# Routing of token tiles and the first part's scatters moved into the attention's slots

## The reference

```python
h = tokens(x, W, b, gamma, beta)                 # 36 patch tokens an image: shifted patches, linear, layer norm; width 192
h = concatenate([h, weight[x_txt]], axis=1)      # 68 tokens an image, 2176 in all
h = h + attention(layernorm(h))                  # 12 heads, each query keeps its 32 best keys
n = layernorm(h)
logits_fk = (n @ W_fk + b_fk) @ normed(emb_fk).T # 128 experts
logits_rk = (n @ W_rk + b_rk) @ normed(emb_rk).T # 128 experts
w_fk, w_rk = top 4 of softmax(logits), divided by their sum
g = sum over the 4 experts e of w_fk[e] * (n @ f_know[e])      # 192 -> 128
y = sum over the 4 experts e of w_rk[e] * (g @ r_know[e])      # 128 -> 192
return h + y
```

## Time and profile before

| | |
|---|---|
| median of 3 executions | 988.81 us (983.92 to 992.14) |
| the profiled execution | 984.25 us, of it the span of the trace 982.4 us |
| TensorE busy, weight loads | 794.3 us (81%), 643.7 us (66%) |
| VectorE | 677.0 us (69%) |
| ScalarE | 324.5 us (33%) |
| GpSimd | 553.8 us (56%) |
| mean granted TensorE clock | 0.847 of 2.4 GHz |
| moved by DMA | 177.19 MB, 180 GB/s in the mean |

### The profile page before, as it was taken

How to read it: one execution, slowest core, us unless ns; L and a number is a source line. 1 busy time by engine, 2 the same in 40 slices (tenths; PEclk the granted TensorE clock), 3 DMA queues, 4 the chain that set the end, 5 groups by cost and what they waited for, 6 DMA issues and landing times.

```text
span 982.4 us, 21622 instructions
## 1 busy us (share of the span) xinstructions
PE 794.3 (81%) x6343; PEld 643.7 (66%) x6343; DVE 677.0 (69%) x4161; ACT 324.5 (33%) x887; POOL 553.8 (56%) x764
## 2 busy tenths in 40 slices
PE   5789999999999999988662288899998699589800
PEld 3778888888888777755441266799976458455800
DVE  2199999999999999984788179885453254255423
ACT  0134334444444344434631011233321146434700
POOL 5256566665666565643547475004775777775075
PEclk9789889998999789975755579999997799889955
DMA  9233453534343346301372496456799798489533
GB/s 331 93 135 129 161 184 112 180 127 163 129 168 114 112 136 219 122 23 34 93 183 71 143 289 226 154 141 176 208 393 409 266 317 297 142 293 367 180 100 92
DMA packets 81578, 177.19 MB, mean 180 GB/s; under 512 B 12952, under 2 KB 38232, under 8 KB 78648
## 3 DMA queue, kind: packets, MB, share of 16 engines
q1 hardware_dynamic: 56088, 120.62, 37.1%
q10 hardware_dynamic: 14112, 32.12, 8.8%
q0 software_dynamic: 11264, 23.09, 7.6%
HBM read 94.25 MB, written 81.53 MB: 179 GB/s over the span
## 4 chain that ended last, share of the span: by engine, by line
DVE 34%; PE 28%; POOL 17%; issue 13%; DMA 5%; ACT 1%; SPq 1%; POOLq 0%; DVEq 0%; ACTq 0%
DVE work L1356 12%; DVE top L1350 9%; PE bank L1216 6%; POOL early L742 5%; PE bank L1199 4%; PE bank L1214 4%; POOL slots_g L749 3%; POOL slots_x L720 3%; PE bank L1264 3%; PE bank L1266 2%; DMA early<-slots_x 2%; DVE s_hit L1520 2%; PE bank L1250 2%; PE bank L965 1%; DVE place L1626 1%
## 5 line engine op out<-in xcount | busy, mean ns | idle before, releaser
L1356 DVE MATCH_REPLACE8 work<-top,work 128x68 f32<-128x68 f32 x896 | 179.3, 211 | 0.0
L1350 DVE MAX8 top<-work 128x8 f32<-128x68 f32 x896 | 128.9, 213 | 6.6 <-ACT tru L792 6.2
L1626 DVE COPY place<-bank 96x512 f32<-96x512 f32 x98 | 66.0, 685 | 82.3 <-PE bank L1199 81.6
L742 POOL DMA_INDIRECT early<-slots_h,s_all x68 | 65.6, 964 | 87.4 <-DMA slots_h<-m_y 67.0
L1635 DVE COPY place<-bank 128x256 f32<-128x256 f32 x98 | 40.9, 423 | 92.8 <-PE bank L1250 91.5
L965 PE MATMUL bank<-early,xp 128*128 128x192 f32 x432 | 94.0, 381 | 6.5 <-DMA xp<-in_a_x 5.0
L965 PEld LDWEIGHTS bank<-early,xp 128*128 128x128 f32 x432 | 90.5, 233 | 8.6 <-DMA xp<-in_a_x 5.3
L742 POOL DMA_INDIRECT early<-slots_y,s_all x68 | 66.3, 975 | 52.7 <-DMA slots_y<-m_y 30.5
L1199 PE MATMUL bank<-ident,early 128*96 128x128 f32 x392 | 68.2, 301 | 25.4 <-DMA early<-slots_x 25.4
L672 POOL TENSOR_TENSOR sc<-work,tru 128x476 f32<-128x476 f32 x32 | 38.0, 1189 | 87.5 <-ACT work L827 87.5
L720 POOL DMA_INDIRECT slots_x<-early,s_all x68 | 67.7, 996 | 31.6 <-issue 18.4
(11 more groups left out here) (187 smaller groups left out, 1729.5 us busy)
## 6 DMA issues: line engine op xcount, KB each, us to landing
early<-slots_x SPq DMA_DIRECT2D x49, 384.0 KB
slots_y<-m_y ACTq DMA_DIRECT2D x49, 384.0 KB
slots_h<-m_y ACTq DMA_DIRECT2D x49, 256.0 KB
early<-slots_g SPq DMA_DIRECT2D x49, 256.0 KB, 4.8
f_all<-in_f_know SPq DMA_DIRECT2D x16, 768.0 KB, 9.8
r_all<-in_r_know SPq DMA_DIRECT2D x16, 768.0 KB, 15.3
slots_x<-zero SPq DMA_DIRECT2D x28, 360.0 KB, 3.0
slots_x<-zero SPq DMA_DIRECT2D x28, 336.0 KB, 3.3
```

The lines of the kernel that those rows point to most:

```text
L742: nc.gpsimd.indirect_dma_start(g_in[:, i % DEPTH, k, 0:width], None, src, bass.IndirectOffsetOnAxis(s_all[:, r - 1, i, k:k + 1], 0)).then_ ...
L1350: last = nc.vector.max(top8[:, c, :], work[:, par, c, :])
L1356: last = nc.vector.match_replace(work[:, par, c, :], top8[:, c, :], work[:, par, c, :], TAKEN)
L1626: nc.vector.tensor_copy(m_flat[u][0:HALF, :], turn_bank[u][0:HALF, :]).then_inc(sem["m_xt0"], 1)
```

## The change

Part 0 is now routed, searched and scattered inside the attention.

- `LOAD_AT` gives tile i of 0 to 14 a slot: 5, 7, 9, ..., 33. Its load and statistics stand there, norm, transposes and query in the slot behind, logits, choice, one-hot and exponentials two behind, its position three behind. Tile 14 (`TAIL`) ends behind the slots; tiles 15 and 16 follow.
- Part 0's counts are taken in slot 24 (`BASE_AT`), base and tile names in 25 to 27. Its searches stand in slots 26 to 30, the first with one tile, the others with two at once; `find_slots(r, i, n)` does n tiles with wider instructions. Its scatters stand in slots 27 to 33 (tiles 5 and 6 together in slot 32), and tile 8's behind the slots.
- Tiles 15 and 16 and the counts of part 1 are made beside the first product of part 0 (`route_beside` on TensorE and ScalarE, a list by group on VectorE). VectorE's searches there are: groups 12 to 15 two tiles of part 1 each for product one, groups 16, 18, 20, 22 two tiles and 24 one tile of part 0 for product two. Part 1's eight for product two move into the first product of part 1. Part 1's scatters, 32 DMAs, follow on GpSimd beside the product of part 0.
- The embedding puts eight products into each slot to the end, so the last stands in slot 20, and the products without use begin in slot 22.
- The product of part 0 takes matrices 7 to 14 first, then 0 to 6, then 15, then the spill; the chunks of `f_all` are loaded in slots 22 to 29 (7 to 14), 0 and 1 behind the attention, 2 to 6 and 15 beside the first groups.
- The position is one product on a running count (`first_row`, fp32, 256 columns) and one with a triangle, instead of two with triangles that add up in one bank. The first product has three PSUM banks in turn, not four. The tiles' small buffers exist twice, the second set (tile 14 on) carved from memory that the embedding's weights held; VectorE's marks of tile 14 wait until all scatters of part 0 have landed. The zeroing of the slot tensors has an order, `slots_x` first.

The diff, cut to what the prediction speaks of:

```diff
-FIRST, LAST = 4, 24
+FIRST, LAST = 4, 22
-SEARCH = 11
-LATE = 13
+LATE = 15
 EARLY = 7
-    EMBED_AT.setdefault(_n // 8 if _n < 48 else 6 + (_n - 48) // 7, []).append((2 + _n // CHUNKS_K, _n % CHUNKS_K))
+    EMBED_AT.setdefault(_n // 8, []).append((2 + _n // CHUNKS_K, _n % CHUNKS_K))
+TAIL = 14
+NEEDS = tuple(((i + 1) * P - 1) // S for i in range(NT))
+LOAD_AT = {}
+for _i in range(TAIL + 1):
+    LOAD_AT[max(NEEDS[_i] + 4, max(LOAD_AT, default=-2) + 2)] = _i
+SLOT_OF = {i: b for b, i in LOAD_AT.items()}
+BASE_AT = SLOT_OF[PARTS[0][1] - 1] + 3
+FIND_AT = {BASE_AT + 2: ((0, 1),), BASE_AT + 3: ((1, 2),), BASE_AT + 4: ((3, 2),), BASE_AT + 5: ((5, 2),), BASE_AT + 6: ((7, 2),)}
+SEND_AT = {BASE_AT + 3: (0,), BASE_AT + 4: (1,), BASE_AT + 5: (2,), BASE_AT + 6: (3,), BASE_AT + 7: (4,), BASE_AT + 8: (5, 6), BASE_AT + 9: (7,)}
...
-            return main + spill if g == 0 else spill + main
+            return main[EARLY:LATE] + main[:EARLY] + main[LATE:] + spill if g == 0 else spill + main
...
@@ sync
+                if b in LOAD_AT:
+                    load_h1(LOAD_AT[b])
...
-            for c in range(EARLY):
+            for c in range(2):
                 load_f(c)
...
-                if g == 0:
-                    sp.wait_ge(sem["weights_known"], 1)
-                    sp.wait_ge(sem["tiles_known"], 1)
                 for n in range(PART_GROUPS[g]):
-                    if g == 0 and LATE + n < CHUNKS:
-                        load_f(LATE + n)
+                    if g == 0 and 2 + n < EARLY:
+                        load_f(2 + n)
+                    if g == 0 and n == EARLY:
+                        sp.wait_ge(sem["t_pos"], TAIL)
+                        sp.wait_ge(sem["tiles_known"], 1)
+                        load_f(LATE)
@@ gpsimd, slot
+                if b - 2 in LOAD_AT:
+                    t_one_hot(LOAD_AT[b - 2])
+                if b in LOAD_AT:
+                    t_rstd(LOAD_AT[b])
+                for i in SEND_AT.get(b, ()):
+                    send(i)
...
+            slot(BATCH + 1, 1)
+            for i in range(TAIL + 1, NT):
+                t_rstd(i)
+            send(8)
+            for i in range(TAIL, NT):
+                t_one_hot(i)
+            for i in range(*PARTS[1]):
                 send(i)
@@ tensor, slot
                 if front:
                     queries_keys(b + 1, 1 - par)
+                if b - 2 in LOAD_AT:
+                    t_logits(LOAD_AT[b - 2])
+                if b - 3 in LOAD_AT:
+                    t_position(LOAD_AT[b - 3])
...
                 for t, k in EMBED_AT.get(b, ()):
                     embed(t, k)
-                if LAST_EMBED < b < BATCH:
-                    keep_busy()
+                if b - 1 in LOAD_AT:
+                    t_turn(LOAD_AT[b - 1])
+                if LAST_EMBED + 1 < b < BATCH:
+                    keep_busy(b)
...
                 if attended:
                     project_out(b - 2, (m + 2) % 4)
+                if b - 1 in LOAD_AT:
+                    t_query(LOAD_AT[b - 1])
+                if b == BASE_AT:
+                    count_part(0)
+                if b == BASE_AT + 1:
+                    sum_counts(0)
+                if b == BASE_AT + 2:
+                    name_tiles(0)
@@ vector, slot
                     nc.vector.tensor_reduce(smax[:], sc1[:, 1 - par], AX.X, ALU.max).then_inc(sem["smax_done"], 1)
+                if b == BASE_AT + 1:
+                    form_counts(0)
+                if b == BASE_AT + 2:
+                    form_base(0)
+                if b == BASE_AT + 3:
+                    take_tiles(0)
                 if take:
                     take8(b, par, 1)
+                if b - 2 in LOAD_AT:
+                    t_choose(LOAD_AT[b - 2])
...
                 if take:
                     take8(b, par, 2)
+                if b in LOAD_AT:
+                    t_stats(LOAD_AT[b])
+                for i, n in FIND_AT.get(b, ()):
+                    find_slots(0, i, n)
                 if take:
                     take8(b, par, 3)
@@ vector, first product
-            beside(turned_first, 0, range(NT + PARTS[1][1] - PARTS[1][0]), find)
-            beside(turned_first, 1, range(*PARTS[0]), first_sum)
+            for n in range(PART_GROUPS[0]):
+                turned_first(FIRST_GROUP[0] + n)
+                if n in (4, 5):
+                    t_choose(TAIL + n - 3)
...
+                if n in (12, 13, 14, 15):
+                    find_slots(0, PARTS[1][0] + 2 * (n - 12), 2)
+                if n in (16, 18, 20, 22, 24):
+                    first = (n - 16) // 2 * 2
+                    find_slots(1, first, min(2, PARTS[0][1] - first))
...
+                if n % 2 == 0:
+                    find_slots(1, PARTS[1][0] + n, 2) if n < 8 else None
+            beside(turned_first, 1, range(*PARTS[0]), sum_and_find)
```

More of the change, by code:

```diff
@@ L215, in build @@
         r_all = nc.alloc_sbuf_tensor_at("r_all", [P, NE, D], F32, offset=shared_from)
+        top = sb("top", [P, NT, 2, 8])
+        t_four = sb("t_four", [P, 2, 2, 8])
+        t_nm = sb("t_nm", [P, NT, 2])
+        idx = sb("idx", [P, NT, 2, 8], U32)
+        e_all = top[:, :, :, K4:2 * K4]
+        e_sum = sb("e_sum", [P, NT, 2])
+        z_all = sb("z_all", [P, NT, 2])
+        ntile_i = sb("ntile_i", [P, 2, 2], I32)
+        ntile = sb("ntile", [P, 2])
+        ends = sb("ends", [P, 4])
+        ended = sb("ended", [P, sum(SPILLS)])
         place = sb("place", [P, 2, NT, NE])
@@ L904, in keep_first @@
                     act.wait_ge(sem["m_mm0"], pair + 1)
-                    made = bank[2 + pair % 4]
+                    made = bank[2 + pair % 3]
                     if first_order(g)[n] < PART_MAIN:
@@ new lines, in t_turn, with t_query @@
+            def t_turn(i):
+                pe.wait_ge(sem["t_norm"], i + 1)
+                if i <= TAIL:
+                    pe.wait_ge(sem["t_placed"], done_by(i, 2))
+                for c in range(2):
+                    last = nc.tensor.transpose(routed_in(i)[0:HALF, c * P:(c + 1) * P], xn_of(i)[:, c * HALF:(c + 1) * HALF], ident[:])
+                last.then_inc(sem["t_turn"], 1)
+            def t_query(i):
+                pe.wait_ge(sem["t_xt"], i + 1)
+                for c in range(2):
+                    last = nc.tensor.matmul(routed_in(i)[:, 0:P], w_rt[:, c, :], t_xT[tail(i)][0:HALF, i % 2, c, :], start=(c == 0), stop=(c == 1))
+                last.then_inc(sem["t_qmm"], 1)
@@ L1217, in multiply_first @@
                 last.then_inc(sem["m_mm0"], 1)
+                route_beside(pair)
             def first_product(g, n, pairs, own):
@@ new lines, in form_base @@
+            def form_base(g):
+                st = part_steps[g]
+                first, end = PARTS[g]
+                mine = base[:, 2 * g:2 * g + 2]
+                nc.vector.tensor_copy(idf[:, first:end], idx[:, first:end, :, 0:K4])
+                dve.wait_ge(sem["base_products"], 3 * g + 2)
+                st.done(nc.vector.tensor_tensor(mine, bank_of_base(g)[:, 0:2 * NE].rearrange("p (q n) -> p q n", q=2),
+                                                iota_e[:].unsqueeze(1).to_broadcast([P, 2, NE]), ALU.subtract))
+                st.done(nc.vector.tensor_copy(ends[:, 2 * g:2 * g + 2], bank_of_base(g)[:, 2 * NE:2 * NE + 2]))
+                st.wait()
+                st.done(nc.vector.tensor_scalar(mine, mine, float(HALVED), float(HALVED * (NE - 1)), ALU.mult, ALU.add))
+                st.wait()
+                for q in range(2 * g, 2 * g + 2):
+                    last = nc.vector.tensor_scalar(ended[:, SPILL_AT[q]:SPILL_AT[q] + SPILLS[q]], iota_t[:, 0:SPILLS[q]], ends[:, q:q + 1], None, ALU.is_ge)
+                st.done(last)
```

685 lines of the change are left out of this document (340 added, 345 removed).

## The result

The change made the kernel slower: median 1012.53 us (1003.84 to 1014.76, 4 executions) against 988.95 us (983.92 to 992.14) for the kernel before, a ratio of 1.023 with a 95% interval of 1.015 to 1.030, which is clear of the noise but leaves open whether it is over 2%. The profiled execution took 1014.76 us, its span 1013.0. The forecast was 967 with a range of its own of 955 to 979, and the highest time that the prediction reckoned with, outside rival 3, was 987.

The account below looks back on a forecast made before the run. VectorE nearly fills the attention, and later work hangs on part 0's first product's end: add at 495.0 + 32.9 + 120.2 = 648.1 us, 20.8 earlier; the rest stays, giving 963.4 profiled, 967 as median, range 955 to 979.

Parts of the forecast that it names:

- rival 3: Attention: granted clock falls, 4.1 us per low-clock slot; nine such slots give 1004 us, slower than before; chance 0.08.
- DVE's added work: Attention: statistics and choices 29.7 us, searches 20.3, small instructions 2.7; 52.7 us in all.
- Even slots of the attention: TensorE's added work makes some eleven even slots run over by 0.3 us each, 3.3 us; odd slots win it back.
- the upper bound of 75 us: Attention's growth, put at 56 us, if every even slot runs over by 1.5 us and nothing is won back.
- POOL's 3.3 us in slot 31: Attention's end: scatters keep POOL about 18 us where DVE needs 13.4, so the next masked add is late by 3.3 us.
- Rival 4: Attention: POOL paces slots 27 to 31 at some 18 us, five slots by 2 us, total 977; chance 0.10.
- Add to first transpose: From the last masked add to part 0's first product: POOL's own order gives the length, 32.9 us.
- Part 0's product: First product of part 0 grows from 110.3 to 120.2 us, with bounds of 106 and 135.
- The rest: After part 0's first product: 313.5 us, unchanged; up to 5 us more if the cover of part 1's scatters fails.
- the 9 us that POOL's chain had to spare: Part 1's product: PE ended at about 768, second product waited to 777 us for POOL, so searches there cost nothing.
- Rival 2: Products: searches of 4.3 us starve PE, 135 instead of 120 us and 5 more in part 1, total 987; chance 0.13.
- The last step of the sum: Whole kernel: 963.4 us profiled becomes 967 in the median, which was 0.46% above the profiled execution before.

Follow-up runs that it names:

- e1: Changed kernel with VectorE's choice of the top experts moved behind the attention output o and the next statistics; 1001.95 us, ratio 1.010 to the kernel before.
- e9: Changed kernel with the choice behind o and eight single searches in part 1's first product; 980.89 us, ratio 0.993 to the kernel before.
- e10: As e9, with the nine sums in part 1's product up to one group sooner; 979.2 us, ratio 0.990 to the kernel before.
- e2: Changed kernel with 12 small products without use on TensorE in slots 5 to 21, ahead of the output's transposes; 1003.12 us, ratio 1.016.
- e3: Changed kernel without the ten products without use in slots 22 to 31; 1017.61 us, ratio 1.026 to the kernel before.
- e6: Changed kernel with choice behind o, 12 small products without use in slots 5 to 21, twenty in 22 to 31, single searches in part 1's product; 992.8 us.
- e11: Changed kernel with part 0's searches and scatters moved behind the last slot, routing left in the slots; 1048.27 us, ratio 1.055.
- e4: Changed kernel with eight single searches, on groups without a sum, for four double ones in part 1's first product; 991.69 us, ratio 1.002.
- e12: As e10, with 20 small products without use in slots 9, 15, 21 and 18 large for 10 in 25, 27, 29; 977.56 us, ratio 0.990.

## Why the prediction was wrong, point by point

- **DVE's added work**, 52.7 us: right, 54.2.
- **Even slots of the attention**, "I charge 0.3 us for each of some eleven even slots, 3.3 us": this step failed, and with it the upper bound of 75 us. It cost about 32 (64.8 measured for the routing, less 29.7 and 2.7). I had added up DVE's work and PE's over the stage and let odd slots win back what even ones lose. They don't: DVE's choice, its statistics and the embedding's norm fall together in slots 9, 15 and 21 (DVE 15.5 to 16.5 us busy), PE is the longer one in the slots behind, and the stage is at least the sum of the longer of the two. I did not look at where the choice stands in DVE's list, ahead of o, though TensorE's transposes and the next scores wait for o: that order alone was 11 to 14 us (e1, e9). The rest, 14.7 us by e9's last add against 495.0, was not taken apart by a run of its own, and its cause stays open. The trace of e9 says only where it lies: in the windows from one masked add to the next, the longer engine makes 429.9 of 449.7 us, 59.3 more than before, and the time in which a slot is longer than either is 19.8 us, 14.4 more than before. In e10's attention, which has the same order, DVE is idle for 32 us, 20 more than before.
- **Rival 3**, the granted clock, had 0.08 and was a part of the cause that I should have priced: with the clock at 0.97 in place of 0.88 the attention was 10.1 us shorter though TensorE did more (e2), and with 0.54 in place of 0.72 it was longer though TensorE did less (e3). But it was not the whole, as e6 shows, and its trigger was told too simply. The Trainium skill, TensorE: Matmul & The Clock Gate, section "HAM oscillation — how this bites in real kernels", has gaps of idle time as what drops the clock. The waits for o and the 4.09 us behind a double search agree with it; e3's 0.54, with PE shown busy for 185.6 of 195 us, does not, and the measurement decides.
- **POOL's 3.3 us in slot 31**: right in kind and about in size. The last add stands at once behind the scatters, with no idle time ahead of it, and slot 31 took 16.3 us where it took 12.3 without scatters (e11):

```profile
522.43 0.96 POOL L723 DMA_INDIRECT slots_x<-early,s_all  x1 [0.30 <-issue]
523.42 1.19 POOL L733 TENSOR_TENSOR sc<-work,tru 128x476 f32<-128x476 f32 x1
```

  Rival 4, such a loss in slots 27 to 30 too, is not seen. Ahead of the adds of slots 29 and 31 GpSimd waited 2.35 and 2.70 us for its input. Those of slots 28 and 30 stand at once behind scatters as well, but ScalarE had finished their input only 0.1 us before, and VectorE did not wait for them.
- **Add to first transpose**, 32.9 us: right, 32.7.
- **Part 0's product**, 120.2 us: the sum right, 118.6, with luck in it. By the starts of the groups' transposes, groups 0 to 11 took 47.2 us where the sum had 53.7, groups 12 to 15 took 22.4 for 22.0, and the spill groups 49.0 for 44.5: two terms were off by 6.5 and 4.5 us in opposite directions. Part 1's scatters started at 612.0 beside it and were done 21 us before it ended.
- **The rest**, "In part 1's product four double searches stand beside DVE's sums; ... I charge nothing": this step failed, by 27.4 us up to the second product. I held the 9 us that POOL's chain had to spare against DVE's time, and not against what a search of 4.3 us behind a sum of 1.4 does to an engine with one pair in hand: in the last and longest case 4 us idle, then 20 us at half the clock, then late sums. Rival 2 had this effect, but with 5 us for part 1. Size and place of the pieces were the matter, not the amount: as singles away from the sums the same work cost 24.5 us less (e4). Which of the two it was is not shown.
- **The last step of the sum**: 963.4 us and 0.46% make 968, not 967. The slip changes nothing.

With both orders mended the sum holds from the attention on: first transpose to second product was predicted as 120.2 + 108.6 = 228.8 us, and took 228.5 in e9.

## What to carry to other kernels

Where two engines take turns at being the longer one, add up the longer of the two slot by slot, as a lower bound; busy times of a stage don't tell its length. When work is put into a full slot, find the chain that sets the slot (here o, transposes, scores) and put it behind the last instruction of that chain on its engine; and put it in pieces shorter than what the fed engine has in hand, away from other pieces. Before products without use are added, mend the order: with it mended the fill was worth nothing here (e12), or cost 12 us (e6 against e9).

## What the runs showed of the hardware

An instruction of VectorE on two columns took 1.56 us in slot 25, and a copy 1.03 us, beside GpSimd's tensor operations:

```profile
404.30 1.56 DVE L1519 TENSOR_SCALAR ntile<-ntile_i 128x2 f32<-128x2 int32 x1
405.89 1.03 DVE L1521 COPY ntile_b<-ntile 128x256 f32<-128x256 f32 x1
```

```profile
404.14 1.69 POOL L645 TENSOR_TENSOR qbd<-qk,head_mask 96x408 f32<-96x408 f32 x2 [0.83 <-ACT qk L818]
405.79 0.98 POOL L744 TENSOR_TENSOR sc<-sc,smax 128x476 f32<-128x476 f32 x1
```

With GpSimd idle the same two lines took 0.17 and 0.29:

```profile
596.16 0.17 DVE L1519 TENSOR_SCALAR ntile<-ntile_i 128x2 f32<-128x2 int32 x1
596.36 0.29 DVE L1521 COPY early<-ntile 128x256 f32<-128x256 f32 x1
```

Each ended with the GpSimd instruction beside it (405.86 and 405.83; 406.92 and 406.77). That is what the Trainium skill says in SBUF — State Buffer, section "SBUF: two separate sides", of a port pair held as an exclusive lock. The other way round, scatters held up by a full VectorE, was hardly seen: over the whole run they took 1.00 us in the mean, as before, and the longest of those in the slots took 1.30 us, where the longest was 1.16 before.

In e3 TensorE stayed at 1.2 GHz from 353 us to the end of the attention, shown busy for 173.0 of 179.0 us:

```profile
353.00:532.00 179.00, 173.03 (x924) 139.41 (x923) 153.94 (x1155) 62.40 (x173) 102.10 (x152) 0.50 0.32 100
```
